# Cutting the expert groups of a two-layer mixture-of-experts kernel differently: 2, 3, 3 and 5, 3 steps in place of 4, 4

## The chip, the cores and the metric

One Trainium2 chip, and one of its cores. The metric is the device time of one execution in microseconds (us); lower is better. Engines are named as in the profile: PE is TensorE, DVE is VectorE, ACT is ScalarE, POOL is GpSimd, SP is SyncE, which computes nothing here and issues most of the DMA transfers.

## The reference

The input is x of 8 x 512 tokens of width 128 (4096 tokens, 32 tiles of 128). Three residual stages follow each other:

```
x = x + 0.5 * ffn(layernorm(x))
x = x + attention(layernorm(x))
x = x + 0.5 * ffn(layernorm(x))
```

ffn normalises its input again, with a scale and a shift, computes 8 router logits per token and picks the two largest; their softmax gives two gates. Each token's output is the gated sum of two of eight routed experts (silu(h Wg) * (h Wu), inner width 384, then Wd back to 128) plus a shared expert of inner width 128. The same weights serve both ffn stages, called layer 0 and layer 1 here. Attention works in windows of 128 tokens, that is inside one tile: q, k, v with biases, scores divided by sqrt(128), of each row only the 32 largest scores are kept, softmax, the product with v, a leaky ReLU (slope 0.01), a residual and a layernorm with gamma and beta. All is in float32.

## The kernel before, in words

**Steps.** The 32 tiles are worked in `STEPS` = 8 steps of `TB` = 4 tiles. Everything but the routed experts goes by steps: the first norms, the routing of layer 0, attention, the routing of layer 1, the shared expert, and the joining of results to x (`combine`, `join`). Since a window is a tile, attention of a step needs that step alone.

**Groups and blocks.** Which expert a token goes to is known only on the chip. A token's normalised row is scattered to DRAM (tensor `rows`) twice, once for each chosen expert, by an indirect DMA of POOL (`scatter`: 8 DMAs a step). Each group of steps has its own part of `rows`, with a region for each expert. A running count `run` gives each token its place. When a group is complete, `region_ends` and `block_list` on DVE turn the counts into two tables, `tab_r` and `tab_w`: for each block its first row and its expert's place among the weights. A block is 128 rows of one expert. A group of n steps holds 8n tiles' worth of rows, and 8 experts can leave at most 7 more blocks part-filled, so its list has 8n + 7 blocks (`NB`, 39 for 4 steps); entries that are not needed point to spare rows and are computed like the others. `fill_all` writes zero rows behind each region's end. `GROUPS` = (4, 4) is used in both layers, so there are four phases (`PHASES`), and 156 blocks in all.

**A block** is cut into four parts (`block_parts`). Part 0: SP loads its rows (`xin`, L380) and its expert's weights (`ws`, L383), PE turns the rows (L585), ACT scales them, POOL copies their numbers to `idx`. Part 1: PE does the gate product (L591), ACT the silu. Part 2: PE the up product (L596), DVE multiplies both (L1188). Part 3: PE the down product (L606), ACT copies it (L779), POOL scatters it to DRAM (`results`, L1385). A part 4 turns one expert's weights, eight times in all, before the first block.

**The order of the work is written by hand.** Each engine runs a fixed program. The step's work is in the loops of its function; between its pieces stands `turn()`, a `Weave` that takes the next count from the strings in `WEAVE` and issues so many block parts there. So the strings say, for each engine apart, at which place of the step's work which block part stands; the engines then wait for each other through semaphores. `turn.rest()` issues what is left. SP's queue is ordered in the same way: loads of rows and weights, `fill_all`, `stored` (a wait until all results of a phase are in DRAM), `results` (a load of one step's results to `yg`, L410) and `output`. `begin(ph)` waits for the list, the fillings and the scatters of the group before the first load of rows of a phase.

**Layer 0.** DVE norms step 0, then steps 1 to 3, then 4 to 7 (`first_stats`, `first_norms`), and routes each step (`route`). The block list of group 0 stands behind the routing of step 3.

**Attention and layer 1** run as a pipeline of three stages over ten turns s of the main loop (`stages`): scores of step a = s, mixing of step A = s - 1, routing for layer 1 of step J = s - 2. In turn s, PE also turns the rows of the next step (`following`, `turn_x`) and projects them, for the next turn to start with; DVE combines the expert results of step s + 2 at the end of turn s and prepares its norms. DVE's `search` finds the 32 largest scores by four rounds of max and replace, with the other DVE work laid between its instructions (`between`). Layer 1's list of group 0 stands behind J = 3, which is turn 5; that of group 1 behind J = 7, turn 9, the last.

**End.** The results of the last group are loaded into `yg_last` and joined (L1120), and the last tiles go out.

## Time and profile before

| what | value |
|---|---|
| median of 3 runs (lowest to highest) | 676.91 us (670.46 to 678.27) |
| the profiled execution's own time; its span | 675.55 us; 673.4 us |
| PE busy | 521.6 us, 77% of the span |
| DVE busy | 406.3 us, 60% |
| POOL busy | 349.1 us, 52% |
| ACT busy | 293.2 us, 44% |
| mean granted clock of TensorE | 0.874 |
| one block product on DVE (L1188) | 551 to 552 ns, 156 of them |
| one indirect DMA on POOL: scatter (L1357), block result (L1385) | 980 ns x128, 986 ns x156 |
| copy of a block's row numbers (L1380) | 202 ns x156 |
| the chain that ended last | PE 41%, issue 13%, DVE 13%, DMA 11%, POOL 10%, SP's queue 7% |

The span runs from the first to the last instruction. Busy shares are averages over stages that are limited by different engines, so the rows below are mostly windows of time and single instructions with their start. PEclk in tenths is the share of its full clock that TensorE was granted. "Idle before <- X" in brackets is how long the engine sat idle ahead of an instruction, and what released it. Block numbers are not in the trace: they come from counting the transposes at L585, one for each block, from 0.

### The profile page before, as it was taken

How to read it: one execution, taken by the hardware profiler on the slowest of the kernel's cores; microseconds unless marked ns; L12 is line 12 of the kernel's file. 1: busy time of each engine (PE TensorE's matmuls, PEld its weight loads, DVE VectorE, ACT ScalarE, POOL GpSimd, SP SyncE). 2: the span in 40 equal slices, each digit the busy share in tenths (PEclk: the TensorE clock that was granted, in tenths of full speed). 3: DMA queues.
4: the chain of work that ended last, by engine and by line, in shares of the span. 5: the costliest groups of instructions: out<-in, count | busy, mean ns of one | idle time of the engine just before them, and what ended most of it. 6: DMA issues, size and time to landing. Idle time of an engine off the chain costs nothing.

```text
span 673.4 us, 14760 instructions
## 1 busy us (share of the span) xinstructions
PE 521.6 (77%) x3795; PEld 463.1 (69%) x3795; DVE 406.3 (60%) x1814; ACT 293.2 (44%) x675; POOL 349.1 (52%) x498
## 2 busy tenths in 40 slices
PE   1686788799989999986075756289899978899980
PEld 1464577689988888886045433278788878899970
DVE  4667877222227789971579997869886712532215
ACT  1232145445544568563041524174654644355530
POOL 2245777775544435457006244227878784455550
PEclk9786599999999999989555757599999899899995
DMA  7911274677768743532302001344455576987736
GB/s 203 296 40 36 80 244 143 204 256 263 246 203 291 236 150 136 189 126 76 101 0 65 0 32 42 132 141 151 164 191 180 167 251 228 319 277 250 249 118 191
DMA packets 78750, 112.23 MB, mean 167 GB/s; under 512 B 11304, under 2 KB 51888, under 8 KB 78672
## 3 DMA queue, kind: packets, MB, share of 16 engines
q1 hardware_dynamic: 65344, 90.04, 39.9%
q0 software_dynamic: 9344, 19.62, 9.0%
q10 hardware_dynamic: 3984, 1.65, 0.9%
q8 instruction: 35, 0.57, 0.4%
q14 instruction: 43, 0.35, 0.2%
HBM read 26.10 MB, written 23.81 MB: 74 GB/s over the span
## 4 chain that ended last, share of the span: by engine, by line
PE 41%; issue 13%; DVE 13%; DMA 11%; POOL 10%; SPq 7%; ACT 3%; ACTq 1%; POOLq 0%; DVEq 0%
PE ps_g L591 9%; PE ps_y L606 9%; POOL rows L1357 5%; PE ps_h L596 4%; PE ps_u L596 4%; DMA xin<-rows 4%; DVE xres L1120 4%; POOL results L1385 3%; DMA raw_dn<-in_dnw 3%; SPq L348 2%; PE w L536 2%; SPq L383 2%; PE ps_s L510 2%; SPq L380 2%; PE ps_x L585 2%
## 5 line engine op out<-in xcount | busy, mean ns | idle before, releaser
L1385 POOL DMA_INDIRECT results<-raw_gu,idx x156 | 153.8, 986 | 150.3 <-ACT raw_gu L779 108.2
L1357 POOL DMA_INDIRECT rows<-zz,s_idx x128 | 125.5, 980 | 42.5 <-issue 28.3
L591 PE MATMUL ps_g<-x_t,raw_dn 128*128 128x128 f32 x936 | 135.1, 282 | 9.8 <-issue 9.7
L606 PE MATMUL ps_y<-dn_t,raw_gu 128*128 x936 | 133.9, 280 | 5.9 <-ACT raw_gu L779 5.2
L591 PEld LDWEIGHTS ps_g<-x_t,raw_dn 128*128 128x128 f32 x936 | 119.5, 195 | 13.2 <-issue 12.9
L606 PEld LDWEIGHTS ps_y<-dn_t,raw_gu 128*128 128x128 f32 x936 | 118.8, 194 | 11.5 <-issue 10.9
L779 ACT COPY raw_gu<-ps_y 128x128 f32<-128x128 f32 x156 | 41.4, 266 | 130.9 <-PE ps_y L606 127.8
L1188 DVE TENSOR_TENSOR raw_gu<-sil,ps_h 128x384 f32<-128x384 f32 x78 | 43.0, 551 | 85.3 <-PE ps_h L596 84.2
L1188 DVE TENSOR_TENSOR raw_gu<-sil,ps_u 128x384 f32<-128x384 f32 x78 | 43.0, 552 | 82.6 <-PE ps_u L596 76.9
L774 ACT ACTIVATE sil<-ps_g 128x384 f32<-128x384 f32 x156 | 76.6, 491 | 29.5 <-PE ps_g L591 26.1
L770 ACT ACTIVATE x_t<-ps_x,bf_c,gf_c 128x128 f32<-128x128 f32 x156 | 72.3, 464 | 33.4 <-PE ps_x L585 32.9
L596 PE MATMUL ps_h<-x_t,raw_dn 128*128 128x128 f32 x468 | 66.1, 278 | 2.7 <-DVE raw_gu L1188 2.7
L585 PE MATMUL ps_x<-ident,xin 128*128 128x128 f32 x156 | 44.1, 283 | 30.2 <-DMA xin<-rows 28.0
L596 PE MATMUL ps_u<-x_t,raw_dn 128*128 128x128 f32 x468 | 67.1, 281 | 0.1
L596 PEld LDWEIGHTS ps_h<-x_t,raw_dn 128*128 128x128 f32 x468 | 59.5, 194 | 4.7 <-DVE raw_gu L1188 3.3
L596 PEld LDWEIGHTS ps_u<-x_t,raw_dn 128*128 128x128 f32 x468 | 60.5, 197 | 0.8 <-issue 0.5
L585 PEld LDWEIGHTS ps_x<-ident,xin 128*128 128x128 f32 x156 | 22.6, 145 | 35.6 <-issue 31.3
L1120 DVE SCALAR_TENSOR_TENSOR xres<-yg,gates,xres 128x128 f32<-128x128 f32 x96 | 31.8, 403 | 21.3 <-DMA yg<-results 21.2
L712 ACT ACTIVATE nz_t<-w,bf_c,gf_c 128x512 f32<-128x512 f32 x16 | 12.5, 778 | 67.9 <-PE w L491 66.1
L1364 POOL TENSOR_TENSOR rg<-rn,ga_b 128x512 f32<-128x512 f32 x8 | 10.3, 1292 | 60.7 <-ACT rn L737 60.7
L1380 POOL COPY idx<-xin 128x1 int32<-128x1 int32 x156 | 31.4, 202 | 18.7 <-PE ps_x L585 18.1
L491 PE MATMUL w<-ident,zz 128*128 128x128 f32 x64 | 14.0, 360 | 32.3 <-DVE zz L962 31.6
(157 smaller groups left out, 793.4 us busy)
## 6 DMA issues: line engine op xcount, KB each, us to landing
raw_dn<-gu_t SPq DMA_DIRECT2D x156, 384.0 KB
xin<-rows SPq DMA_DIRECT2D x156, 64.5 KB
yg<-results SPq DMA_DIRECT2D x12, 512.0 KB, 5.0
results<-raw_gu,idx POOLq DMA_INDIRECT x156
rows<-pads SPq DMA_DIRECT2D x32, 64.5 KB
rows<-zz,s_idx POOLq DMA_INDIRECT x128, 2.3
raw_gu<-results SPq DMA_DIRECT2D x4, 512.0 KB, 5.5
raw_dn<-in_dnw SPq DMA_DIRECT2D x1, 1536.0 KB, 17.2
```

The source lines that it names most:

```text
L585: pe.transpose(ps_x[:, 0, :], xin[:, k4, 0:D], ident[:]).then_inc(xT_ps, 1)
L591: t = pe.matmul(ps_g[:, c, :], ws[:, k4, c * P:(c + 1) * P], x_t[:, k, :], start=True, stop=True)
L596: t = pe.matmul(ps_us[k][:, c, :], ws[:, k4, FF + c * P:FF + (c + 1) * P], x_t[:, k, :], start=True, stop=True)
L606: t = pe.matmul(ps_y[:, 0, :], h_t[:, k4, c * P:(c + 1) * P], dn[:, bass.ds(off + c * D, D)], start=(c == 0), stop=(c == FC - 1))
L770: act.activation(x_t[:, k, :], ps_x[:, 0, :], ACT.Identity, bias=bf_c[:], scale=gf_c[:]).then_inc(xT_sb, 1)
L774: act.activation(sil[:, k, :], ff(ps_g), ACT.Silu).then_inc(sil_done, 1)
L779: act.copy(yb[:, k4, :], ps_y[:, 0, :]).then_inc(y_sb, 1)
L1120: dve.scalar_tensor_tensor(res(tile, k), y[:, k, c, :], gates[:, c, bass.ds(tile + k, 1)], res(tile, k), ALU.mult, ALU.add).then_inc(cb, 1)
L1188: dve.tensor_tensor(h_t[:, k4, :], sil[:, k, :], ff(ps_us[k]), ALU.mult).then_inc(h_done, 1)
L1357: pool.indirect_dma_start(xs, bass.IndirectOffsetOnAxis(s_idx[n][:, c, k:k + 1], 0), zz[n][:, k, c, :], None).then_inc(scat[n], 16)
L1380: pool.tensor_copy(idx[:, k8:k8 + 1], xin[:, k4, D:D + 1].bitcast(I32)).then_inc(idx_cp, 1)
L1385: pool.indirect_dma_start(yt, bass.IndirectOffsetOnAxis(idx[:, k8:k8 + 1], 0), yb[:, k4, :], None).then_inc(yst[k4], 16)
```

## The change

The groups become (2, 3, 3) steps in layer 0 and (5, 3) in layer 1, so there are five groups (`NG`). A group may be listed in pieces: `LISTS` gives the steps behind which a list is made. In layer 1 these are steps 3, 5, 7 and 8. A list made while its group is still growing takes only blocks that are full by then: 8 experts can hold back at most 7 part-filled blocks, so at least 8n - 7 are full, and just so many are listed. `listed` keeps how many of each expert were taken, and the next list of the group starts behind them. A phase (`PHASE`) is now one list. Their block counts are 23, 31, 31 and 17, 30, 9, 22: 163 in all.

In the attention pipeline, turns 2 and 5 are `LATE`: their steps begin a group of layer 0. For these the turn ahead doesn't prepare the rows; DVE combines, norms and scales them at the end of the turn (`before`, `rows_now`), and PE and ACT turn and project them at the start of turns 2 and 5. The first norms go in four chains (`FIRST_CHAINS`) instead of three. The DMAs that zero the spare rows move from POOL to SP, behind the loads of the weights, and are five instead of two. At the end, three steps are joined from `yg_last` instead of four. All five strings of `WEAVE` are new.

The diff, cut to its core:

```diff
-GROUPS = (4, 4)
-NG = len(GROUPS)
-STEPS = sum(GROUPS)
+STEPS = 8
+GROUPS = ((2, 3, 3), (5, 3))
+LISTS = ((2, 5, 8), (3, 5, 7, 8))
+NG = sum(len(g) for g in GROUPS)
+FIRST_CHAINS = (0, 1, 2, 5, STEPS)
+LATE = (2, 5)
...
-FROM = sums(GROUPS)
 SPARE = NE - 1
-NB = tuple(2 * TB * n + SPARE for n in GROUPS)
-FIRST = sums(NB * 2)
-REGION = tuple(TB * n * P + P for n in GROUPS)
+Phase = namedtuple("Phase", "layer group steps at lo hi blocks first last")
+def phases():
+    group = 0
+    for layer in range(2):
+        for lo, end in itertools.pairwise(sums(GROUPS[layer])):
+            listed, at = 0, lo
+            for to in (n for n in LISTS[layer] if lo < n <= end):
+                last = to == end
+                upto = 2 * TB * (to - lo) + (SPARE if last else -SPARE)
+                yield Phase(layer, group, end - lo, at, lo, to, upto - listed, at == lo, last)
+                listed, at = upto, to
+            group += 1
+PHASE = tuple(phases())
+PHASES = len(PHASE)
+FLUSHES = sums(p.last for p in PHASE)
+FIRST = sums(p.blocks for p in PHASE)
+STEPS_OF = tuple(p.steps for p in PHASE if p.last)
+REGION = tuple(TB * n * P + P for n in STEPS_OF)
 ROWS = tuple(NE * r + SPARE * P for r in REGION)
 ROW0 = sums(ROWS)
 GROUP_ROWS = -(-ROW0[-1] // NG)
...
-(WEAVE: the counts of block parts at each place, five strings)
+(WEAVE: five other strings)
...
-        FIRST_NORMS = 3
+        FIRST_NORMS = len(FIRST_CHAINS) - 1
...
-            return s + 1 if s + 1 < STEPS else None
+            return s + 1 if s + 1 < STEPS and s + 1 not in LATE else None
...
-            for n in range(GROUPS[0]):
-                tokens(n * TB, (n + 1) * TB, ld_x[n])
-            tokens(GROUPS[0] * TB, NT, ld_x[GROUPS[0]])
+            for n, (lo, hi) in enumerate(itertools.pairwise(FIRST_CHAINS)):
+                tokens(lo * TB, hi * TB, ld_x[n])
...
+            sp.wait_ge(pad_z, 1)
+            sp.wait_ge(cst, 1)
+            for g in range(NG):
+                at = ROW0[g] + NE * REGION[g]
+                sp.dma_start(xs[at:at + SPARE * P].rearrange("(s p) d -> p s d", p=P), pads[:, NE:, :]).then_inc(spare, 16)
...
-                sp.wait_ge(padded, (ph + 1) * (16 * NE))
-                apart(sp)
-                l, g = divmod(ph, NG)
-                for J in range(FROM[g], FROM[g + 1]):
-                    R = l * STEPS + J
+                if PHASE[ph].last:
+                    sp.wait_ge(padded, FLUSHES[ph + 1] * (16 * NE))
+                    apart(sp)
+                for J in range(PHASE[ph].at, PHASE[ph].hi):
...
-            fill_all(0)
-            for ph in range(1, NG):
-                fill_all(ph)
-            for g in range(NG):
-                stored(g)
-                for J in range(FROM[g], FROM[g + 1]):
-                    results(J, J % 2, J * TB)
-            for g in range(NG):
-                fill_all(NG + g)
-            for g in range(NG - 1):
-                stored(NG + g)
-                for J in range(FROM[g], FROM[g + 1]):
-                    results(STEPS + J, J % 2, J * TB)
-                    if J:
-                        output(STEPS + J - 1, J * TB - TB)
-            output(STEPS + FROM[NG - 1] - 1, FROM[NG - 1] * TB - TB)
+            flushes = [ph for ph in range(PHASES) if PHASE[ph].last]
+            for layer in range(2):
+                here = [ph for ph in flushes if PHASE[ph].layer == layer]
+                for ph in here:
+                    fill_all(PHASE[ph].group)
+                for ph in here:
+                    if ph == flushes[-1]:
+                        break
+                    stored(ph)
+                    for J in range(PHASE[ph].lo, PHASE[ph].hi):
+                        results(layer * STEPS + J, J % 2, J * TB)
+                        if layer and J:
+                            output(STEPS + J - 1, J * TB - TB)
+            F = PHASE[-1].lo
+            output(STEPS + F - 1, F * TB - TB)
...
-            turn_x(0, 0, STEPS, first=True)
-            turn()
-            queries(0)
-            turn()
-            keys(0, None, STEPS)
-            turn()
...
+                if s == 0 or s in LATE:
+                    turn_x(s % XRING, s, done)
+                    turn()
+                    queries(s)
+                    turn()
+                    keys(s, None, done)
+                    turn()
...
-            def block_list(ph, g):
-                N, nb, nt = 12, NB[g], TB * GROUPS[g]
-                chained, n = links(bl, ph * N)
...
+                f = PHASE[ph]
+                g, nb, nt = f.group, f.blocks, TB * (f.hi - f.lo)
+                chained, n = links(bl, links_of_lists[0])
...
-                link(dve.tensor_tensor(cnt[:], run[:], region(g), ALU.subtract))
+                if f.last:
+                    link(dve.tensor_tensor(cnt[:], run[:], region(g), ALU.subtract))
+                else:
+                    link(dve.scalar_tensor_tensor(cnt[:], run[:], -float(P - 1), region(g), ALU.add, ALU.subtract))
...
+                if not f.first:
+                    link(dve.tensor_tensor(nbk[:], nbk[:], listed[:, 0:NE], ALU.subtract))
...
+                if not f.last:
+                    link(dve.tensor_scalar(upto[:, 1:NE + 1], bend[:], float(nb), None, ALU.min))
+                    if f.first:
+                        link(dve.tensor_tensor(listed[:, 0:NE], upto[:, 1:NE + 1], upto[:, 0:NE], ALU.subtract))
+                    else:
+                        link(dve.tensor_tensor(more[:], upto[:, 1:NE + 1], upto[:, 0:NE], ALU.subtract))
+                        link(dve.tensor_tensor(listed[:, 0:NE], listed[:, 0:NE], more[:], ALU.add))
+                links_of_lists[0] += n[0]
...
+            def after_step(layer, J):
+                for ph in range(PHASES):
+                    f = PHASE[ph]
+                    if (f.layer, f.hi) == (layer, J + 1):
+                        if f.last:
+                            region_ends(f.group)
+                        block_list(ph)
+                        if f.last and f.group + 1 < NG:
+                            start_group(f.group + 1)
...
+            def first_chain(n):
+                lo, hi = FIRST_CHAINS[n], FIRST_CHAINS[n + 1]
+                for J in range(lo, hi):
+                    first_stats(J)
+                first_norms(n, lo * TB, hi * TB)
+            def first_rows(R):
+                norm_z(R, R, R * TB, R * TB, used=False)
...
+            first_chain(1)
             for R in range(STEPS):
-                if R == 0:
-                    for J in range(1, G0):
-                        first_stats(J)
-                    first_norms(1, TB, G0 * TB)
-                if R + 1 < STEPS:
-                    norm_z(R + 1, R + 1, (R + 1) * TB, (R + 1) * TB, used=False)
+                chain = FIRST_CHAINS.index(R + 1) if R and R + 1 in FIRST_CHAINS[:-1] else None
+                if chain is None and R + 1 < STEPS:
+                    first_rows(R + 1)
                 route(R)
-                if R == 1:
-                    for J in range(G0, STEPS):
-                        first_stats(J)
-                    first_norms(2, G0 * TB, NT)
+                if chain is not None:
+                    first_chain(chain)
+                    first_rows(R + 1)
             dve.wait_ge(ld_c, 16 * 5)
             gates_of_layer(0)
             dve.wait_ge(gts, 1)
...
+            def before(p):
+                combine(p, p % 2, p * TB)
+                stats_before(p, p * TB)
+            def rows_now(p):
+                J = next(chains)
+                for m in range(N_NORM):
+                    norms(m, J, p, None)
+                    turn()
+                norm_x(p % XRING, p * TB)
+            before(0)
+            rows_now(0)
+            if 1 not in LATE:
+                before(1)
             for s in range(STEPS + 2):
                 (a, A, Jr), p = stages(s), following(s)
...
-                if Jr is not None and Jr + 1 in FROM:
-                    g = FROM.index(Jr + 1) - 1
-                    region_ends(NG + g)
-                    block_list(NG + g, g)
-                    if g + 1 < NG:
-                        start_group(NG + g + 1, g + 1)
-                if s + 2 < STEPS:
-                    combine(s + 2, s % 2, (s + 2) * TB)
-                    stats_before(s + 2, (s + 2) * TB)
+                if Jr is not None:
+                    after_step(1, Jr)
+                if s + 1 in LATE:
+                    before(s + 1)
+                    rows_now(s + 1)
+                if s + 2 < STEPS and s + 2 not in LATE:
...
-            pool.wait_ge(pad_z, 1)
-            for g in range(NG):
-                at = ROW0[g] + NE * REGION[g]
-                pool.dma_start(xs[at:at + SPARE * P].rearrange("(s p) d -> p s d", p=P), pads[:, NE:, :]).then_inc(spare, 16)
```

## Rows read from the trace of the kernel before

**Rows 1.** the page's forty slices: TensorE's granted clock in tenths, GB/s moved
```profile
PEclk9786599999999999989555757599999899899995
...
GB/s 203 296 40 36 80 244 143 204 256 263 246 203 291 236 150 136 189 126 76 101 0 65 0 32 42 132 141 151 164 191 180 167 251 228 319 277 250 249 118 191
```

**Rows 2.** windows by stage: span, busy us (count) of PE, PEld, DVE, ACT, POOL
```profile
87.00:165.00 78.00, 67.64 (x566) 63.53 (x566) 34.88 (x108) 39.11 (x91) 56.73 (x83) 1.00 0.67 225
...
310.00:431.50 121.50, 59.98 (x233) 40.98 (x231) 94.58 (x527) 32.30 (x62) 45.11 (x47) 0.61 0.14 42
...
256.90:299.10 42.20, 38.27 (x296) 34.97 (x295) 38.80 (x200) 28.13 (x65) 21.70 (x29) 0.96 0.44 149
...
354.60:382.00 27.40, 17.34 (x65) 12.23 (x66) 25.30 (x149) 10.66 (x19) 10.34 (x12) 0.62 0.14 40
...
382.00:412.30 30.30, 19.43 (x66) 12.73 (x66) 26.51 (x149) 10.66 (x19) 12.86 (x13) 0.56 0.05 18
...
412.30:456.90 44.60, 26.34 (x163) 22.37 (x163) 34.58 (x169) 18.19 (x36) 17.09 (x21) 0.78 0.36 119
```

**Rows 3.** PE timeline (start, us): block turns, tail and phase change
```profile
615.80 0.27 PE L585 MATMUL ps_x<-ident,xin 128*128 128x128 f32 x1
...
617.92 0.27 PE L585 MATMUL ps_x<-ident,xin 128*128 128x128 f32 x1
...
556.09 0.27 PE L585 MATMUL ps_x<-ident,xin 128*128 128x128 f32 x1
...
569.32 0.27 PE L585 MATMUL ps_x<-ident,xin 128*128 128x128 f32 x1
```

**Rows 4.** chain of waits, PE: last scatter, block 0, last expert
```profile
81.47 2.30 DMA rows<-zz,s_idx
...
86.94 0.30 PE L585 MATMUL ps_x<-ident,xin 128*128 128x128 f32 x1
...
55.18 0.49 PE L566 MATMUL ps_h<-ident,raw_dn 128*128 128x128 f32 x3
```

**Rows 5.** POOL timeline: step 2 begins, last scatter, two block results
```profile
60.56 0.20 POOL L1349 COPY zz<-result_no 128x8 int32<-128x8 int32 x1 [5.36 <-DVE s_idx L1033]
...
140.64 0.98 POOL L1357 DMA_INDIRECT rows<-zz,s_idx  x1 [0.16 <-issue]
...
143.26 0.98 POOL L1385 DMA_INDIRECT results<-raw_gu,idx  x1 [0.16 <-issue]
...
144.60 0.97 POOL L1385 DMA_INDIRECT results<-raw_gu,idx  x1 [0.16 <-issue]
```

**Rows 6.** PE and DVE in order of time: marks of the attention steps
```profile
204.51 1.66 DVE L1120 SCALAR_TENSOR_TENSOR xres<-yg,gates,xres 128x128 f32<-128x128 f32 x6 [1.92 <-DMA yg<-results]
...
214.68 0.60 PE L482 MATMUL w<-ident,xn 128*128 128x128 f32 x4
...
220.38 1.06 PE L525 MATMUL w<-k_t,q_t 128*128 128x128 f32 x8
...
251.98 0.60 PE L482 MATMUL w<-ident,xn 128*128 128x128 f32 x4
...
431.55 0.45 PE L585 MATMUL ps_x<-ident,xin 128*128 128x128 f32 x1 [12.65 <-DMA xin<-rows]
```

**Rows 7.** chain of waits round 321: landing of results, their sums
```profile
321.71 4.79 DMA yg<-results
...
326.53 2.20 DVE xres L1120 x8
```

**Rows 8.** PE and DVE in order of time: the last block, the last joins
```profile
647.59 0.27 PE L585 MATMUL ps_x<-ident,xin 128*128 128x128 f32 x1
...
662.18 8.49 DVE L1120 SCALAR_TENSOR_TENSOR xres<-raw_gu,gates,xres 128x128 f32<-128x128 f32 x32 [10.38 <-DMA raw_gu<-results]
```

**Rows 9.** SP's queue in order of time: filling transfers of one group
```profile
415.66 4.50 SPq L394 DMA_DIRECT2D rows<-pads  x8
```

**Rows 10.** waits over the span: us in total, times, longest
```profile
DVE xres L1120 <- DMA yg<-results: 21.2, 4, 13.8
```

More of the change, by code:

```diff
@@ L12 @@
 import itertools
+from collections import namedtuple
 from contextlib import ExitStack
@@ L234, in macaron @@
         nbk = sb("nbk", [P, NE])
+        more = sb("more", [P, NE])
+        listed = sb("listed", [P, NE + 1])
         bend = sb("bend", [P, NE])
+        upto = sb("upto", [P, NE + 1])
         cmp16 = sb("cmp16", [P, NE, MOST_T])
@@ L243, in macaron @@
         tab_r = sb("tab_r", [P, FIRST[-1]], I32)
[L244 removed]
+        ends = sb("ends", [P, NG * NE], I32)
         xin = sb("xin", [P, 4, XW])
@@ L256, in macaron @@
         ld_gu = [sem(f"ld_gu{n}") for n in range(2)]
-        ld_x = [sem(f"ld_x{n}") for n in range(GROUPS[0] + 1)]
+        ld_x = [sem(f"ld_x{n}") for n in range(len(FIRST_CHAINS) - 1)]
         cst, pc, pad_z = sem("cst"), sem("pc"), sem("pad_z")
@@ L273, in macaron @@
         yld = [sem(f"yld{n}") for n in range(2)]
-        yld_last = [sem(f"yld_last{n}") for n in range(GROUPS[-1])]
+        yld_last = [sem(f"yld_last{n}") for n in range(LAST_G)]
         xn_done, xnT_ps, xnT_sb, q_ps, q_sb, k_ps, k_sb, v_ps, v_sb = (
@@ L472, in mix, with turn_x @@
                 t.then_inc(o_ps, 1)
-            def turn_x(n, scored, done, first=False):
+            def turn_x(n, scored, done):
                 pe.wait_ge(xn_done, (scored + 1) * TB)
-                if first:
-                    pe.wait_ge(xr_done, done + 1)
-                else:
+                pe.wait_ge(xr_done, done + 1)
+                if scored:
                     pe.wait_ge(sc_sb, scored)
@@ L841, in _ @@
             turn.rest()
-            for J in range(FROM[NG - 1], STEPS):
+            for J in range(PHASE[-1].lo, STEPS):
                 output(STEPS + J, J * TB)
@@ L1243, in norms @@
                 newton(n, nw, J * N_NW, 0 if p is not None else ROUTE_AT, ROUTE_AT, ROUTE_AT + TB if R is not None else ROUTE_AT)
-            J = next(chains)
-            combine(0, 0, 0)
-            stats_before(0, 0)
-            for m in range(N_NORM):
-                norms(m, J, 0, None)
-                turn()
-            norm_x(0, 0)
-            combine(1, 1, TB)
-            stats_before(1, TB)
+            def before(p):
[5 more added lines that the diff above has]
+                    norms(m, J, p, None)
+                    turn()
+                norm_x(p % XRING, p * TB)
[3 more added lines that the diff above has]
+                before(1)
             for s in range(STEPS + 2):
@@ L1256, in _ @@
                 R, rt = (None, None) if Jr is None else (STEPS + Jr, Jr * TB)
-                J = next(chains)
+                J = next(chains) if p is not None or R is not None else None
                 after = AFTER if a is not None else AFTER_LATE
@@ L1314, in _ @@
         def _(pool):
+            pool.memset(upto[:], 0.0)
+            pool.memset(listed[:], 0.0)
             pool.memset(sel[:], 0.0).then_inc(pc, 1)
```

99 lines of the change are left out of this document (51 added, 48 removed).

## The prediction

> **What bounds the kernel now.** I read the page's forty slices first. TensorE's granted clock is at 8 or 9 tenths in slices 6 to 19, at 5 to 7 in slices 20 to 26, and at 8 or 9 again up to the last but one [rows 1]. The windows by stage say what happens there: from 310.0 to 431.5 us TensorE is busy 59.98 of 121.5 us at a mean clock of 0.61, while VectorE is busy 94.58 [rows 2]. No expert block runs in that stretch: all 78 of layer 0 are through, and none of layer 1 can be listed until step 3 is routed. It is a chain of attention steps, led by VectorE. Elsewhere there are other rates. GpSimd is busy 56.73 of the 78.0 us from 87 to 165 [rows 2]. TensorE repeats a lone block every 2.12 us (615.80 to 617.92), and where a phase changes five blocks take 13.23 us (556.09 to 569.32), so a change costs 13.23 - 10.60 = 2.6 us [rows 3]. The end is a tail behind the last block.
>
> **Block counts.** A group of n steps has 8n + 7 blocks, a partial list 8n - 7. Before: 4 x 39 = 156. After: 23 + 31 + 31 in layer 0, and 17 + 30 + 9 + 22 in layer 1: 85 + 78 = 163. The seven new ones cost 7 x 2.12 = 14.8 us of TensorE and are inside the counts below. I laid the written order of each queue beside the code, block by block; the marks of the new order are timed by intervals of the old.
>
> **Start.** The last scatter of group 0 is issued at 81.47, lands in 2.30, and block 0 is turned at 86.94, 5.5 after the issue [rows 4]. After, block 0 needs steps 0 and 1 alone. Their last scatter ends at 55.2, since GpSimd sits idle 5.36 us ahead of 60.56 [rows 5], so it is issued at 54.2; all experts are turned at 55.7 [rows 4]. Block 0 comes at about 60, 27 us sooner.
>
> **That gain is not kept.** GpSimd scatters steps 2 to 7 in both kernels: 6 x (8 x 1.28 + 1.0) = 67.5 us from 60.6, with 1.34 for a block's result and its number (143.26 to 144.60). Before, 11 results stand among them: 60.6 + 67.5 + 14.7 = 142.8, and the trace has the last scatter at 140.64 [rows 5], so GpSimd is the bound. After, 26 results stand ahead of the last scatter: 140.6 + 15 x 1.34 = 160.7, with a little idle 163. Before, about 27 blocks are through at that time too. What does come sooner is the end of group 0: 23 blocks instead of 39.
>
> **Attention starts sooner, then waits.** The turn of step 0's rows is at 214.68 before, ahead of block 48 [rows 6]. After, it stands ahead of block 31. Result 22 leaves at some 150; 2.3 to land, 4.79 to load results [rows 7], and from the first sum to the turn 204.51 to 214.68 less four block products of 0.55, 8.0 [rows 6], give 165 at the earliest; by the blocks it is 163 + 6 x 2.12 = 175. Steps 0 and 1 take 37.3 us with 11 blocks before (214.68 to 251.98) [rows 6]; after, up to block 39, some 28, so 203. Then 23 blocks (40 to 62) stand alone: 203 + 23 x 2.12 = 252. Step 2 needs block 53: 203 + 14 x 2.12 = 233, + 4 until its result is issued, + 2.3 + 4.8 + 8 = 252. Both meet at 253, where before has 252. So at this mark (turn_x2) the kernel is three blocks ahead and nothing more.
>
> **Steps 2 to 4.** Step 2 takes 42.2 us before, with 12 blocks. Its own TensorE work is about 17.34 x 0.62 = 10.8 us at full clock, and VectorE is busy 25.3 of 27.4 in a step without blocks [rows 2]. After, it carries 8 blocks: 42.2 - 4 x 2.12 = 33.7; VectorE wants 27 + 8 x 0.55 = 31.4; I take 35. Step 3 with 10 blocks: 38. Step 4 has almost none: 30.3 [rows 2], less 1 for the shorter list, and behind it, no longer overlapped, about 4 us of norms and row scaling on VectorE and the 5.7 us from turning rows to scores (214.68 to 220.38) [rows 6]: 39. Scores 5 come at 253 + 5 + 35 + 38 + 39 = 370, against 382.0: 12 sooner. Queued on VectorE behind the new list of 17 blocks (some 3 us) is the whole of step 5; it is in the 39.
>
> **Steps 5 and 6.** Blocks 85 to 101 can be listed now, where before had none until 431.55 [rows 6]. They lie over steps 5 (9 blocks) and 6 (7): 42.2 - 3 x 2.12 = 36, and 34 (VectorE: 27 + 4 + a list), against 30.3 and 44.6. Scores 7 come at 370 + 70 = 440, against 456.9: 17 sooner, with 102 blocks of 163 done (61 left) where before had 85 of 156 (71 left).
>
> **To the last block.** Block 102 waits for step 4's scatter: in the old trace the first block starts 19.3 us after the scores of the next step (412.3 to 431.55), so 459. Blocks 102 to 162 are 60 intervals, 127.2 us; TensorE's own work for routes 5 to 7 (5 each: 10.8 less some 6 of a step without route) and the last mixing is 19.5; two phase changes 5.2. Waits: before, from 456.9 to 647.59 [rows 8], 190.7 less 71 x 2.12 = 150.5, less 21 of own work, less 2.6, leaves 16.6; I take 16. 459 + 127.2 + 19.5 + 5.2 + 16 = 627, against 647.59.
>
> **Tail.** 673.4 - 647.6 = 25.8 us. The last joins are 32 in 8.49 us [rows 8]; three steps have 24, so 2.1 less: 23.7.
>
> **Sum.** Span 627 + 24 = 651, plus the 2.15 us by which the profiled execution's own time (675.55) exceeds its span (673.4): 653. That execution stands 1.4 under the median of the runs, 676.91; 653 is 22.5 us under the one, 24 under the other.
>
> **Costed at nothing.** Lists in layer 0: VectorE idles there behind GpSimd; uncovered, some 3 us each. Eight more filling transfers: eight are issued in 4.50 us [rows 9], between loads that run ahead; uncovered, 4.5. The two new fills with zeros on GpSimd lie ahead of the first weights. The transfers of spare rows go from GpSimd to SyncE, behind three weight loads, and are five instead of two: 5 x 7 x 128 rows x 516 bytes = 2.31 MB. Bounds: 0 where they run in free time (slices 3 and 4 move 36 to 40 GB/s), 7.8 us where block 0 waits for all of it at slice 2's 296 GB/s [rows 1]. I take 0: the first fill is only due at about 44, and GpSimd's backlog would swallow a late block 0.
> The Trainium skill, "DMA: Bandwidth & Descriptors", section "Queues, rings and completion order", says that each DMA engine takes a queue's descriptors in ring order: the fills would then stand behind the spare rows. No row here shows it. By that rule block 0 could slip by up to those 7.8 us, and the end by less.
>
> TensorE's clock is 0.56 to 0.62 in the steps without blocks and 0.96 in step 2 [rows 2]; my steps 2, 3, 5 and 6 are already taken from the latter. The Trainium skill, "TensorE: Matmul & The Clock Gate", section "What's actually happening", says that recent activity opens the clock; the trace agrees, with 0.61 in the hole. By it the change could lose nothing there.
>
> **Rivals.**
> A, more than forecast: the 16 us of waits are mostly those of TensorE restarting after the hole and do not come back, and step 4 runs near full clock: 653 - 12 - 3 = 638. For it: blocks run up to the scores of step 6. Against: TensorE now runs out of blocks twice.
> B, no measurable change: VectorE's written order, not TensorE, paces the steps, and fewer blocks help nothing. Steps 2 and 3 at 42.2 and step 4 at 43 add 7.2 + 4.2 + 4, so 668. For it: VectorE is busy 38.80 of 42.2 us in step 2 [rows 2]. Against: 12 x 0.55 of these are block products, and four of the twelve go.
> C, slower: the hand-overs. A group's results must be stored, loaded and summed before the next attention step, and SyncE issues rows and results in one order, so later blocks' rows queue behind a wait for stored results. Place: the turns of rows 0, 2 and 5. Price: the longest wait for results before, 13.8 us [rows 10], at each: 41.4, so 694. It decides from some 12.5 us each (690.4 is 2% over the median). Against: the written order keeps several blocks between a group's last result and its use.
> That the change does not do what it says (no block of layer 1 ahead of step 3's routing) is ruled out by the written order; it gets no share.
>
> **Chances.** Forecast 0.60, with a range of its own of 642 to 664; A 0.12; B 0.19; C 0.09. A measurement of this kernel tells about 2% from no change: 663.4 and 690.4. Faster: nearly all of the forecast, and A, 0.71. Within: B, and a little of the forecast and of C, 0.21. Slower: 0.08. The range for 8 in 10 reaches from A to beyond B: 636 to 674.
>
> **What would show it.** Right: block 0 at about 60 but the last scatter of layer 0 at 160 or later; turn_x2 at 253 within 7; scores 5 at 370, scores 7 at 440, the last block turned at 627; 17 blocks of layer 1 between 367 and 435, and the clock over 0.8 there. Wrong: VectorE waiting over 12 us for results at turn_x2 or turn_x5; block 102 later than 470; steps 2 and 3 over 42 us.

## The result, and the profile after

The changed kernel takes **650.6 us** (median of 4 runs, 649.0 to 652.9) against 674.2 us before in the same set (670.5 to 678.3): ratio 0.965, 95% interval 0.958 to 0.973. A later set of six runs gave 652.3, ratio 0.967 (0.965 to 0.970). The profiled execution took 650.28 us with a span of 648.5. The forecast was 653, in 636 to 674.

The page's forty slices, with TensorE's granted clock in tenths, answer to [rows 1]:

```profile
PEclk9965999987899999999997589998599999999995
```

Seven slices in a row at 5 to 7 tenths have become two short dips, at slices 22 and 23 and at 29. The windows by stage (span, then busy us and count of PE, PEld, DVE, ACT and POOL, granted clock, DMA share, GB/s) are those of steps 2 and 3, the two stretches without a new block, and the stretch from block 102 to the last block:

```profile
252.00:331.00 79.00, 73.26 (x575) 66.82 (x574) 67.99 (x344) 47.39 (x110) 43.21 (x60) 0.98 0.49 167
331.10:373.30 42.20, 14.62 (x100) 12.04 (x99) 37.92 (x192) 9.79 (x23) 26.08 (x29) 0.69 0.24 77
424.50:460.00 35.50, 16.24 (x116) 13.21 (x115) 32.88 (x172) 11.78 (x26) 22.08 (x25) 0.85 0.18 56
460.00:624.60 164.60, 147.53 (x1209) 139.25 (x1210) 88.04 (x319) 85.60 (x207) 97.62 (x148) 0.97 0.69 230
```

The stretch of 121.5 us without blocks [rows 2] is cut in two, 42.2 and 35.5 us. VectorE still fills most of each (37.9 and 32.9 us). The 17 blocks of layer 1 that the prediction wanted to see between 367 and 435 are turned from 373.3 to 424.5, at a granted clock of 0.96.

The marks that the prediction set, from the timelines of each kernel:

| mark (us) | before | predicted | after |
|---|---|---|---|
| block 0 turned | 86.9 | 60 | 63.3 |
| last scatter of layer 0 issued | 140.6 | 163 | 167.4 |
| rows of step 0 turned (turn_x0) | 214.7 | 175 | 173.4 |
| turn_x2 | 252.0 | 253 | 259.0 |
| scores 4 | 354.6 | 331 | 329.0 |
| scores 5 | 382.0 | 370 | 378.8 |
| scores 7 | 456.9 | 440 | 440.3 |
| blocks left at scores 7 | 71 | 61 | 61 |
| block 102 | | 459 | 460.0 |
| last block | 647.6 | 627 | 624.6 |
| tail behind it | 25.8 | 23.7 | 23.9 |

The last block and the last joins, from the timeline of the changed kernel, answer to [rows 8]:

```profile
624.62 0.27 PE L618 MATMUL ps_x<-ident,xin 128*128 128x128 f32 x1
...
639.44 6.39 DVE L1187 SCALAR_TENSOR_TENSOR xres<-raw_gu,gates,xres 128x128 f32<-128x128 f32 x24 [10.61 <-DMA raw_gu<-results]
```

VectorE's waits for results (us in total, times, longest), on which rival C rests, answer to [rows 10]: there are more of them, but the longest is shorter. The longest is ahead of row 0; the one ahead of row 2, from VectorE's timeline, stands below it, and there is none ahead of row 5.

```profile
DVE xres L1187 <- DMA yg<-results: 18.3, 7, 8.5
...
248.45 0.61 DVE L1187 SCALAR_TENSOR_TENSOR xres<-yg,gates,xres 128x128 f32<-128x128 f32 x2 [2.56 <-DMA yg<-results]
```

### The profile page after: what moved, and what is told of

The parts are those of the page before. It is cut to its first block, busy times and chain, and to the rows that moved or that the text cites. A ratio compares the mean times of both kernels' runs of the same rounds, so it can differ in the third digit from the quotient of the medians.

```text
span 648.5 us, 15350 instructions
## 1 busy us (share of the span) xinstructions
PE 510.9 (79%) x3928; PEld 464.5 (72%) x3928; DVE 426.7 (66%) x1893; ACT 296.5 (46%) x694; POOL 353.7 (55%) x515
## 4 chain that ended last, share of the span: by engine, by line
PE 48%; DMA 13%; issue 11%; POOL 10%; DVE 7%; SPq 6%; ACT 4%; ACTq 1%; POOLq 0%; DVEq 0%
PE ps_g L624 10%; PE ps_y L639 10%; PE ps_u L629 5%; PE ps_h L629 5%; POOL rows L1426 5%; DMA xin<-rows 4%; POOL results L1454 4%; DMA yg<-results 3%; DMA raw_dn<-in_dnw 3%; SPq L383 2%; PE ps_x L618 2%; PE w L569 2%; PE ps_s L543 2%; DVE pr L1239 2%; DVE xres L1187 2%
## 5 line engine op out<-in xcount | busy, mean ns | idle before, releaser
L1454 POOL DMA_INDIRECT results<-raw_gu,idx x163 | 160.3, 984 | 147.7 <-ACT raw_gu L813 88.5
L639 PE MATMUL ps_y<-dn_t,raw_gu 128*128 x978 | 140.3, 281 | 15.8 <-ACT raw_gu L813 15.7
L624 PE MATMUL ps_g<-x_t,raw_dn 128*128 128x128 f32 x978 | 141.0, 282 | 7.4 <-issue 7.4
L639 PEld LDWEIGHTS ps_y<-dn_t,raw_gu 128*128 128x128 f32 x978 | 124.5, 194 | 23.6 <-issue 23.1
L624 PEld LDWEIGHTS ps_g<-x_t,raw_dn 128*128 128x128 f32 x978 | 125.1, 196 | 12.5 <-issue 12.1
L808 ACT ACTIVATE sil<-ps_g 128x384 f32<-128x384 f32 x163 | 79.9, 490 | 28.3 <-PE ps_g L624 27.3
L629 PE MATMUL ps_u<-x_t,raw_dn 128*128 128x128 f32 x492 | 70.3, 281 | 0.0
L618 PEld LDWEIGHTS ps_x<-ident,xin 128*128 128x128 f32 x163 | 23.9, 147 | 50.4 <-issue 43.7
L1223 DVE MAX8 top<-wk_s 128x8 f32<-128x128 f32 x96 | 26.7, 288 | 1.0 <-DVE rstd L956 1.0
L1229 DVE MATCH_REPLACE8 wk_s<-top,wk_s 128x128 f32<-128x128 f32 x96 | 26.4, 276 | 0.0
L909 DVE BATCH_NORM_STATS2 bn<-xres 128x6 f32<-128x128 f32 x96 | 21.5, 280 | 3.3 <-DMA xres<-in_x 2.2
```

The lines of the kernel that those rows point to most:

```text
L618: pe.transpose(ps_x[:, 0, :], xin[:, k4, 0:D], ident[:]).then_inc(xT_ps, 1)
L624: t = pe.matmul(ps_g[:, c, :], ws[:, k4, c * P:(c + 1) * P], x_t[:, k, :], start=True, stop=True)
L629: t = pe.matmul(ps_us[k][:, c, :], ws[:, k4, FF + c * P:FF + (c + 1) * P], x_t[:, k, :], start=True, stop=True)
L639: t = pe.matmul(ps_y[:, 0, :], h_t[:, k4, c * P:(c + 1) * P], dn[:, bass.ds(off + c * D, D)], start=(c == 0), stop=(c == FC - 1))
L808: act.activation(sil[:, k, :], ff(ps_g), ACT.Silu).then_inc(sil_done, 1)
L1454: pool.indirect_dma_start(yt, bass.IndirectOffsetOnAxis(idx[:, k8:k8 + 1], 0), yb[:, k4, :], None).then_inc(yst[k4], 16)
```

## Experiments: the two halves of the change

The change has two halves: smaller groups in layer 0, and lists of growing groups in layer 1. Either half needs an order of its own. For the four kernels below I wrote all five strings of `WEAVE` anew, by one procedure. The first has the groups of the kernel before, the fourth those of the changed kernel, so that the order's own share can be seen.

**Groups of before, new order** (only the strings differ from the kernel before).

> The kernel before with other WEAVE strings and nothing else: groups (4, 4) in both layers, 156 blocks, lists behind complete groups; ACT, DVE, POOL and SP put a block part ahead of step work wherever it can run. Theory (the gain of the change needs the new groups and lists): the stretch without expert blocks, 310.0 to 431.5 us before, stays over 90 us long, and the time stays within 2% of before, 660 to 688 us. Rival (the change gained because its five strings are a better order, not because of its groups): 655 us or less.

**Split only.**

```diff
-GROUPS = ((2, 3, 3), (5, 3))
-LISTS = ((2, 5, 8), (3, 5, 7, 8))
+GROUPS = ((2, 3, 3), (4, 4))
+LISTS = ((2, 5, 8), (4, 8))
```

> The change's code with layer 0 in groups of 2, 3, 3 steps, but layer 1 in 4, 4 and no list of a growing group (85 + 78 = 163 blocks), order by the same rule as e1. Theory (the earlier start of attention is given back at the turn of step 2's rows, and layer 1 cannot be listed before its step 3): 10 to 20 us under e1, of which seven more blocks take back 15; against e1 between -20 and +5. Rival (the split of layer 0 alone makes the gain): 24 us or more under e1, as much as the whole change.

**Growing lists only.**

```diff
-GROUPS = ((2, 3, 3), (5, 3))
-LISTS = ((2, 5, 8), (3, 5, 7, 8))
-FIRST_CHAINS = (0, 1, 2, 5, STEPS)
-LATE = (2, 5)
+GROUPS = ((4, 4), (5, 3))
+LISTS = ((4, 8), (3, 5, 7, 8))
+FIRST_CHAINS = (0, 1, 4, STEPS)
+LATE = ()
```

> The change's code with layer 0 in groups of 4, 4 steps as before, but layer 1 in 5, 3 with the lists behind steps 3, 5, 7 and 8 (78 + 78 = 156 blocks), no LATE turns, order by the same rule as e1. Theory: the first block of layer 1 comes one step earlier (some 28 us before where e1 has it), steps 5 and 6 carry 17 blocks, and the tail behind the last routing has 22 blocks for 39: 15 to 30 us under e1. Rival (the split alone makes the gain): within 7 us of e1.

**Both, new order** (only the strings differ from the changed kernel).

> The changed kernel with other WEAVE strings and nothing else, order by the same rule as e1. Theory: it stands to e1 as the changed kernel to the one before, 20 to 40 us under it, and the sum of the two parts (e2 and e3 against e1) or more, since the work that the split sets free is what the early lists need. Rival (the order is what counts): within 10 us of e1.

| kernel | median us | ratio to before (95%) | scores 7 | blocks left | last block |
|---|---|---|---|---|---|
| before | 674.0 | | 456.9 | 71 | 647.6 |
| e1: old groups | 690.9 | 1.026 (1.019 to 1.033) | 459.7 | 71 | 665.3 |
| e2: split only | 670.1 | 0.994 (0.991 to 0.998) | 443.4 | 71 | 643.7 |
| e3: growing only | 668.0 | 0.992 (0.989 to 0.995) | 459.2 | 61 | 646.3 |
| e4: both | 654.6 | 0.974 (0.968 to 0.980) | 444.0 | 61 | 624.8 |
| changed kernel | 650.6 | 0.965 (0.958 to 0.973) | 440.3 | 61 | 624.6 |

The kernel before and e1 to e4 are of one set; the last row is the result above, from another set. The marks are those of each kernel's profile.

The order alone gains nothing: e1 is slower than the kernel before (690.9 us, outside the 660 to 688 of its forecast), and its stretch without blocks is still 122.7 us long (310.0 to 432.7). e2 is 20.8 us under e1, just past its 10 to 20, e3 23.0, within its 15 to 30, and e4 36.3, within its 20 to 40; but e4's forecast that both together give the sum of the parts or more did not hold (36.3 against 43.8).

The table is clean up to scores 7. The split alone brings scores 7 some 16 us nearer and leaves the same 71 blocks. The growing lists alone leave ten blocks fewer and bring nothing nearer. Together they do both. The medians are less clean: my order for a last group of four steps has a fault that the order of the kernel before has not. Both e1 and e2 have the line below (this is e1's timeline of TensorE) at the change to the last phase, a wait of 15.7 us for rows; before, that change cost 13.23 us for five blocks in all [rows 3].

```profile
577.36 0.45 PE L581 MATMUL ps_x<-ident,xin 128*128 128x128 f32 x1 [15.73 <-DMA xin<-rows]
```

So "-21 us for the split, -23 for the lists, -36 for both" against e1 overstates the lists. The kernel before gets from scores 7 to its last block, over the same 71 blocks, in 190.7 us, where e1 takes 205.6 and e2 200.3. With 190.7 for both (worked out, not run) they would stand at 676 and 661: the split alone would be worth 15.5 us, the lists alone 8.1, both 21.5. What the runs do show: each half alone in my order beats the kernel before by under 1%, and both together by 2.6%; and the lists are worth 15.5 us on top of the split (e2 to e4), of which up to 9.6 may be that fault.

## Experiments: what paces the opening

**GpSimd made longer.** In each of steps 2 to 6 of layer 0:

```diff
                 number(R, R % RING, R * TB)
+                if 2 <= R <= 6:
+                    for k in range(4):
+                        pool.memset(rg[:], 0.0).then_inc(pc, 1)
+                        pool.wait_ge(pc, 4 + 4 * (R - 2) + k + 1)
```

> The changed kernel with GpSimd made longer in the opening: in each of steps 2 to 6 of layer 0 four extra 128x512 memsets of a scratch tile ahead of the eight scatters, about 0.45 us each by the 204 ns of a 128x128 one, 9 us in all. Theory 1 (my sum): GpSimd's scatters and block stores pace layer 0 until its last scatter, which lands at 167.4 us, so that this comes 7 to 9 us later, turn_x0 with it, and the kernel ends 5 to 9 us later, at 655 to 660. Theory 2: VectorE's routing or TensorE paces the opening and GpSimd has slack there: the end moves by less than 2 us.

Measured: 660.6 us (658.5 to 663.5) beside 652.3 for the unchanged one in the same set, so 8.3 us longer and just above the 655 to 660 of theory 1; the memsets took 10.7 us, not 9. The added work, in the groups of GpSimd's instructions from 60 to 180 us (count, busy us, mean ns, idle time before):

```profile
L1463 POOL MEMSET rg<- 128x512 f32 x20 | 10.7, 533 | 1.6 <-POOL zz L1418 0.8
```

The last scatter of layer 0, in GpSimd's timeline of the same kernel:

```profile
176.95 0.98 POOL L1426 DMA_INDIRECT rows<-zz,s_idx  x1 [0.16 <-issue]
```

10.7 us were put in, the last scatter came 8.8 us later than in the unchanged kernel's profile of that set (168.17), turn_x0 8.7 (182.7 against 174.0) and the end 8.3. GpSimd paces layer 0, as the forecast had it, and nothing later takes the loss back. What paces is the work that GpSimd has in all, not the mark of the last scatter by itself: e2 and e4 put 36 block results ahead of the last scatter instead of 26, it comes at 184.6 and 183.0 us, and turn_x2 still comes at 252.9 and 251.0, sooner than in the changed kernel.

**Spare rows on GpSimd again.** This undoes a part that I had costed at nothing:

```diff
 (SyncE, behind the weight loads)
-            for g in range(NG):
-                at = ROW0[g] + NE * REGION[g]
-                sp.dma_start(xs[at:at + SPARE * P]..., pads[:, NE:, :]).then_inc(spare, 16)
 (GpSimd, ahead of its first scatter)
+            pool.wait_ge(pad_z, 1)
+            for g in range(NG):
+                at = ROW0[g] + NE * REGION[g]
+                pool.dma_start(xs[at:at + SPARE * P]..., pads[:, NE:, :]).then_inc(spare, 16)
```

> The changed kernel with the five transfers of spare rows (2.31 MB in all) issued by GpSimd again, as in the kernel before, instead of by SyncE behind the weight loads. The prediction costed this move at nothing, between 0 and 7.8 us at block 0. Block 0 was turned at 59.7 to 63.3 us in seven profiles of kernels of this order, where I had 60. Theory 1: free either way, since GpSimd's scatters pace the opening and swallow a late block 0: block 0 within 59 to 64, the last scatter of layer 0 and the end within 1.5 us of the changed kernel (650.6 to 652.3). Theory 2: on SyncE they hold up block 0's rows: block 0 comes 2 us or more earlier, below 59, and the end by up to as much. Theory 3: on GpSimd their issues delay its first scatters: everything up to the last scatter comes 1 to 5 us later, and the end with it, at 652 to 656.

Measured: **661.4 us** (659.6 to 665.8), ratio to before 0.980 (0.976 to 0.984), so 9 to 11 us slower than the changed kernel (9 to 10 by the ratios, as the sets differ). Theory 3 had the sign, but neither the size nor the reason: GpSimd's issues (4.94 us for all five, at 3.8 us) end long before its first scatter. TensorE's timeline of this kernel shows it, at the turning of the experts' weights (the wait, and the last expert):

```profile
39.77 0.90 PE L592 MATMUL ps_g<-ident,raw_gu 128*128 128x128 f32 x3 [10.68 <-DMA raw_dn<-in_dnw]
...
62.00 0.85 PE L596 MATMUL ps_h<-ident,raw_dn 128*128 128x128 f32 x3
```

The same two places in the changed kernel:

```profile
28.07 0.55 PE L595 MATMUL ps_g<-ident,raw_gu 128*128 128x128 f32 x3 [2.33 <-DMA raw_dn<-in_dnw]
...
51.14 0.85 PE L599 MATMUL ps_h<-ident,raw_dn 128*128 128x128 f32 x3
```

Issued at 3.8 us, the 2.31 MB run beside the loads of x and of the weights. In the page's list of transfers the two 768 KB loads of x take 16.3 us to land instead of 9.7. The first expert's turning comes 11.7 us later, and the chain of waits adds that up: the small weights, for which SyncE waits, are in at 12.8 instead of 9.6 us; issuing the first load of expert weights takes 5.35 us instead of 0.86; the load of `raw_dn` lands in 21.4 us instead of 17.5. The experts are all turned at 62.9 instead of 52.0, block 0 comes at 74.1 instead of 60 to 63, the last scatter at 178.9 instead of 167.4 to 168.2. The kernel before had two such transfers (0.92 MB) there; five on GpSimd would have cost the change nearly half of its gain.

The new place isn't free either, and theory 2 has a part of the truth. SyncE waits until the spare rows have landed before it issues the first `fill_all`, and the load of block 0's rows stands behind that. SyncE's waits from 30 to 70 us in the changed kernel (total, times, longest), its timeline, and TensorE's at block 0 in the later run of the same kernel (f0):

```profile
SPq L342 <- DMA rows<-pads: 12.3, 2, 10.4
...
50.76 4.31 SPq L429 DMA_DIRECT2D rows<-pads  x8
...
60.58 0.30 PE L618 MATMUL ps_x<-ident,xin 128*128 128x128 f32 x1 [3.12 <-DMA xin<-rows]
```

Since the kernel itself waits here, no run shows in what order SyncE's queue would have taken the fillings and the spare rows without that wait. The fillings go out at 50.8, where the prediction had them due at 44 and the counts that they need are ready at 34.3. In five of the seven profiles of this order TensorE then idles 1.7 to 4.8 us for block 0's rows. The last scatter doesn't show it: it comes at 166.6 to 168.7 in all seven, with block 0 anywhere from 59.7 to 63.3.

## Experiments: what paces the steps

**The transpose of block 85 moved.** In TensorE's order it stood ahead of the queries of step 5, and waited 4.86 us for the block's rows:

```profile
367.33 1.11 PE L515 MATMUL w<-ident,xn 128*128 128x128 f32 x4 [15.53 <-DVE xn L987]
373.30 0.45 PE L618 MATMUL ps_x<-ident,xin 128*128 128x128 f32 x1 [4.86 <-DMA xin<-rows]
...
378.81 1.06 PE L558 MATMUL w<-k_t,q_t 128*128 128x128 f32 x8
```

First it was moved behind the keys, then (g1) everything of blocks 85 and 86 behind scores 5. The counts of block parts at these places:

```diff
 turn_x5, queries5, keys5, scores5     (the changed kernel)
-PE  1 0 3 0     ACT  1 0 2 0
+PE  0 0 4 0     ACT  0 0 3 0          (f1_turn_behind_keys)
+PE  0 0 0 4     ACT  0 0 0 3          (g1_behind_scores; VectorE's product of block 85 two places later)
```

> The changed kernel with one part of the hand-written order moved: the transpose of block 85 (the first block of layer 1's second group) and its copy on ScalarE stand behind the keys of step 5 instead of ahead of its queries. Theory 1: step 4 took 49.8 us instead of my 39 partly because TensorE sat 4.86 us at that transpose, waiting for the block's rows, with queries, keys and scores 5 queued behind it; then scores 5 come 4 to 5 us earlier and the kernel ends at 646, between 644 and 648. Theory 2: the stretch is paced by VectorE's list of the second group and its scatters, and the blocks of the group come when they come, so that scores 5 move but the last block does not: 650, within 1.5 us of the baseline.

> The changed kernel with all of blocks 85 and 86 that stood ahead of scores 5 on TensorE (four parts), ScalarE (three) and VectorE (one product, behind which the first maximum of the step's search stood) moved right behind scores 5. Moving only the part ahead of queries 5 brought scores 5 no more than 1.0 us nearer to their turn of rows (11.48 to 10.46 us), since the wait for rows then stood ahead of the scores. Theory 1: turn to scores is 5 to 6 us now, as in steps 0 and 1, scores 5 come 5 us earlier, and so does all behind them: 645 to 647 against the changed kernel's 650.6 to 652.3. Theory 2: TensorE has 61 blocks behind scores 7 either way and GpSimd's and SyncE's queues pace them: scores 5 to 7 come 5 us earlier, the last block less than 2: 649 to 652.

Measured: 649.7 (648.4 to 652.7) and 652.7 us (647.1 to 653.5), against 652.3 (652.0 to 653.5) in f1's set and 650.6 in the first: no difference that can be told. g1 is of another set; by their ratios to before, 0.964 for each against 0.965 and 0.967, they agree too. In f1 the wait only changed its place, since block 86 still stood ahead of the scores. In g1 it is gone, as TensorE's timeline shows:

```profile
367.58 1.12 PE L515 MATMUL w<-ident,xn 128*128 128x128 f32 x4 [13.92 <-DVE xn L987]
...
373.97 2.05 PE L558 MATMUL w<-k_t,q_t 128*128 128x128 f32 x8 [0.82 <-issue]
```

From turn to scores it is 6.4 us now, not 11.5, and step 4 takes 44.8 us instead of 48.3 to 49.8. But step 5 takes 36.1 instead of 30.8, and scores 6 are where they were (410.1 against 410.7). Block 85 is turned as late as before (375.8 against 374.7), and TensorE's work from there paces step 5: it is busy 33.4 of the 36.1 us. So theory 2's time came nearly true (652.7 for 649 to 652), but not its way: scores 6 and 7 don't come 5 us earlier. A step's start that comes sooner isn't worth anything where blocks with a fixed start have to be got through in the step.

**VectorE made longer.** At the start of each search of steps 2 to 7:

```diff
+                if a >= 2:
+                    for k in range(3):
+                        dve.tensor_tensor(wk_s[:], sc[:], sc[:], ALU.add).then_inc(more_dve, 1)
+                        dve.wait_ge(more_dve, 3 * (a - 2) + k + 1)
```

> The changed kernel with VectorE made longer in attention steps 2 to 7: three extra 128x512 additions into a scratch tile, 0.69 us each, at the start of each step's search, 2.1 us a step, 12.4 in all. My forecast had VectorE pace only the step in the hole (4) and the end of 7, and TensorE those with blocks (2, 3, 5, 6): then the steps 4 and 7 get 2 us longer, the others under 1 each, and the kernel takes 653 to 657. Rival B of the prediction (VectorE's written order paces every step): each step is 2 us longer, scores 7 come 10 us later, and the kernel takes 660 to 665.

The 18 additions took 12.5 us. Measured: 655.2 us (654.9 to 657.6), 2.8 over the unchanged kernel (1.9 by the ratios, 0.970 against 0.967, whose intervals overlap). From scores 2 to 7 it takes 179.7 us, where two profiles of the unchanged kernel take 175.4 and 176.3: 3.4 to 4.3 of the 10.4 us put in. Of 2.1 us in each step, step 2 showed 0.7, step 3 0.8, step 5 0.8 to 1.0 and step 6 0.4 to 0.9. Step 4, the one in the hole, took 49.8, and the unchanged kernel 48.3 and 49.8. So rival B, with 10 us by scores 7 and 660 to 665, is out. That VectorE paces step 4 more than the steps under blocks, as my forecast had it, isn't shown by this run.

**The attended rows on VectorE.** `attended` moves from GpSimd's turn to the start of VectorE's next one:

```diff
 (VectorE, in turn s, ahead of stats_route)
+                    attended(Jr, rt)
 (GpSimd)
-                pool.wait_ge(rn_done, A * TB + 2 * TB)
-                pool.tensor_tensor(rg[:], rn[:], wide(ga_b), ALU.mult).then_inc(rg_done, 1)
...
-                pool.tensor_tensor(xr, xr, rg[:], ALU.add).then_inc(x2_done, 1)
```

> The changed kernel with the three 128x512 operations that scale, shift and add the attended rows (gamma, beta, residual) on VectorE, at the start of the next step, instead of on GpSimd, where they take 1.31 us each; on VectorE they should take 0.5 to 0.7 us each, so 1.5 to 2.1 us of its time a step. Theory 1: while they run on GpSimd, VectorE's small operations stretch from 0.28 to 1.3 to 1.75 us, about 4 us a step on the path between two scores; with them moved, steps get 1 to 3 us shorter each and the kernel ends 5 to 15 us earlier, at 636 to 646. Theory 2: the stretched operations lie beside other waits, and VectorE gets 2 us a step more to do on the path: the kernel ends 2 to 12 us later, at 653 to 663.

> The same with the three operations on the attended rows on VectorE instead of GpSimd too, which alone gave 644.9 (ratio 0.956), 7.4 us under the changed kernel beside it: no step between two scores got shorter by it, the gain came behind scores 7, where GpSimd has most to do. If the two gains are of different places they add: 640, between 637 and 643. If both only bring the last stretch's work closer to GpSimd's own bound: 643 to 646.

Measured: **644.9 us** (643.7 to 647.6), ratio to before 0.956 (0.953 to 0.958), 7.4 under the unchanged kernel of its set; with the moves of g1 as well **643.5** (641.3 to 647.7), ratio 0.952 (0.948 to 0.957), so in the 643 to 646 of its second case: the two moves don't add to 640. What led there is seen in the changed kernel. GpSimd's timeline has the three operations, of which these are the first two:

```profile
350.00 1.28 POOL L1433 TENSOR_TENSOR rg<-rn,ga_b 128x512 f32<-128x512 f32 x1
351.36 1.26 POOL L1435 TENSOR_TENSOR rg<-rg,ba_b 128x512 f32<-128x512 f32 x1
```

And VectorE's timeline, at the same time, has `pr` at 1.4 and 1.75 us instead of 0.28. Each of the two ends 0.16 us behind one of GpSimd's:

```profile
349.69 1.75 DVE L1239 SCALAR_TENSOR_TENSOR pr<-wk_s,ex 128x128 f32<-128x128 f32 x1
...
351.38 1.40 DVE L1239 SCALAR_TENSOR_TENSOR pr<-wk_s,ex 128x128 f32<-128x128 f32 x1
```

The view of that one operation gives its min, median and max ns. In the changed kernel the longest of the 32 takes six times the median:

```profile
L1239 DVE SCALAR_TENSOR_TENSOR pr<-wk_s,ex x32: 279/290/1754, 195.7 to 481.3; 128x128 f32<-128x128 f32 x32
```

With `attended` on VectorE none is long:

```profile
L1251 DVE SCALAR_TENSOR_TENSOR pr<-wk_s,ex x32: 278/286/293, 196.6 to 476.7; 128x128 f32<-128x128 f32 x32
```

Eleven of the 32 are long in the changed kernel, 0.8 to 1.75 us, 10.9 us over the median in all; every one of them runs beside one of the three operations, though others beside them take 0.28. That GpSimd's operations stretch VectorE's is shown, but theory 1 had the place of the gain wrong. From scores 2 to 7 this kernel takes 175.1 us, the unchanged one of its set 175.4: what VectorE wins back it spends on the three operations (0.68 to 0.69 us each). The gain lies behind scores 7: to the last block 181.0 instead of 185.4 us, where GpSimd is busy 99 us instead of 109; over the run it is rid of 31.4 us (8 x 3.93). VectorE is hardly less busy there (104.4 instead of 105.4 us), so the gain looks like that of a freed GpSimd, not of shorter operations on VectorE; no run here separates the two. The rest stood at scores 7 already (440.2 against 442.1), as differences that single profiles of one kernel show too. g2 has 180.3 there, and scores 7 at 436.7. The 1.4 us between the two medians, of two sets, lie within their spread.

## Why the prediction was right, and where not

**Start: the time right, by luck.** Block 0 came at 63.3 for 60 (59.7 to 63.3 in seven profiles). I had it 5.5 us behind a last scatter of step 1 issued at 54.2. That scatter is issued at 44.3, ten sooner than I took from the old trace. x of step 0 is there at 5.1 to 5.3 us in either kernel. What lands sooner are the small weights (9.6 for 12.9 us) and the experts' (28.0 for 30.9), and the new order puts step 1's router products ahead of the first expert's turning. With the spare rows back in the old place that scatter is at 57.0. I had costed their move at nothing, with 7.8 us as its largest loss. It is worth 9 to 11 us, as a gain over the same five transfers in the old place. The step that failed is the edit "costed at nothing": I didn't ask what the transfers held up in their old place; and the hold-up in the new one, which I had set at 0, is there too. My number came out since other waits took the ten us: in this profile the last expert (52.0), VectorE's norms of step 2 behind it and step 2's router and shared products on TensorE (55.99 to 63.25), which stand ahead of block 0; in five of the other six profiles block 0's own rows, loaded behind the spare rows.

**"That gain is not kept": right.** GpSimd paces layer 0. I had 163 for the last scatter, measured 167.4 with the 26 results ahead of it that I counted, and 10.7 us added to GpSimd gave 8.3 at the end.

**Turn_x2: 6 late.** 253 foreseen, 259.0 measured. Block 53, the last of the group, was turned at 230.4, 2.6 sooner than my 233. It is the hand-over behind it that I had too short: 8.3 us until its result is issued (238.74; I had 4), 4.6 until SyncE issues the load of results (243.37; 2.3), with the rows of three later blocks and the weights of two ahead of it from 240.1 on, 5.1 to the first sum (4.8), 10.6 from there to the turn (8). That is rival C's mechanism, at a small part of its price. The change between the lists costs more than my 2.6 us as well: from block 22 to 23 it is 12.6 us, 5.9 of them waits for ScalarE's copies of block results, from 53 to 54 7.1; but block 53 was not late by it.

**Steps 2 and 3: right, a little pessimistic.** 30.5 and 34.5 us for 35 and 38, at granted clocks of 0.94 and 1.00. That made good the six.

**Step 4: wrong by 11 us, without effect.** I had 39, it took 49.8: 27.2 from scores to the routing's last index and 3.9 for the list (I had 29.3 for both), 7.3 of joins and norms (I had 4), 11.5 from turn to scores (I had 5.7). The largest is the transpose of block 85 ahead of the queries, which the written order showed and my sum left out. It cost nothing at scores 6, as g1 shows, because step 5 is then paced by TensorE's work from block 85 on. Steps 5 and 6 took 61.5 us instead of my 70: 30.6 for 36, where g1, with blocks 85 and 86 behind scores 5 instead of ahead of it, has 36.1; and 30.9 for 34, the cause of which stays open. So some 5 us of step 4 and step 5 are one thing, counted twice with opposite signs.

**To the last block and the tail: right.** 184.3 us from scores 7 for my 187, with 61 blocks left; block 102 at 460.0 for 459; the tail 23.9 for 23.7, with the joins 6.39 us.

**The sum.** Against the forecast the stretches are off by +6 (to turn_x2), -8 (steps 2 and 3), +11 (step 4), -8 (5 and 6) and -3 (to the last block). One part of this, step 4 against step 5, hangs together; that the rest comes to 2 us is luck. The mechanism, fewer blocks behind scores 7 and scores 7 sooner by 17 us, is right.

**The rivals.** A (638) did not come: waits for rows are still there, 14.3 us at block 102 alone. B is refuted by steps 2 and 3 (30.5 and 34.5 for its 42.2) and by the added VectorE work, of which 3.4 to 4.3 of 10.4 us showed. C's waits for results were 8.6 us at row 0, 2.6 at row 2 and none at row 5, below its 12.5.

**Where the gain sits.** The last block comes 23.0 us sooner: 16.5 at scores 7 (456.86 to 440.34), most of which e2 has by the split alone (13.5), and 6.4 behind it (190.7 to 184.3). There TensorE is busy 151.4 us instead of 176.0, with ten fewer blocks, but idles 32.9 instead of 14.8; 15.8 of these lie between scores 7 and block 102.

## What to carry to other kernels

A transfer that "has time" is costed at the place that it leaves as well as where it goes: 2.3 MB of zeros beside the first loads were worth 9 to 11 us. A stretch that looks late in a trace is not yet a loss; move it alone and see whether the mark behind it moves. And work on an engine that looks idle may be paid by its neighbour: look for one operation's duration having two values.

## What was not expected of the hardware

- VectorE's 128x128 operation `pr` of 0.28 us took 0.8 to 1.75 us in 11 of 32 cases, all beside GpSimd's 128x512 tensor operations, and never more than 0.293 with these gone.
- The same 128x512 addition takes GpSimd 1.3 us and VectorE 0.69 us; a 128x512 memset takes GpSimd 0.53.
- TensorE's clock was granted at half, the lower of its two levels, in the opening too: 0.50 from 45 to 63 us, where it is busy 10.8 of 18.0 us and each expert's three last transposes take 0.85 us instead of 0.49.
